# Second layer of a two-layer convolution kernel: branch bias as matmuls, left pooling read from PSUM, one norm for all of c1

## The reference, cut to what matters

```
x = x + L0(_gn(x), ...)
g = _gn(x)                                    # "input norm" of the second layer
p1 = relu(conv3x3(g, p1_w) + p1_b)            # 64 -> 32 channels, branch 1
p2 = relu(conv3x3(g, p2_w) + p2_b)            # 64 -> 32 channels, branch 2
pool1 = cummax(p1, axis=H, reverse=True)      # top pooling
pool2 = cummax(p2, axis=W, reverse=True)      # left pooling
p_gn1 = group_norm(conv3x3(pool1 + pool2, p_w), p_gn_g, p_gn_b)
gn1   = group_norm(conv1x1(g, c1_w), gn1_g, gn1_b)
x = x + relu(conv3x3(relu(p_gn1 + gn1), c2_w) + c2_b)
```

## Time and profile before

| what | value |
|---|---|
| median of 3 runs | 147.26 us (147.07 to 148.74) |
| profiled execution: own time | 146.71 us |
| profiled execution: span, first to last instruction | 144.9 us |
| PE matmul busy | 126.0 us, 87% |
| DVE busy | 109.3 us, 75% |
| ACT busy | 57.2 us, 39% |
| POOL busy | 19.7 us, 14% |
| mean granted clock of TensorE | 0.986 |

### The profile page before, as it was taken

How to read it: one execution, slowest core, us unless ns; L and a number is a source line. 1 busy time by engine, 2 the same in 40 slices (tenths; PEclk the granted TensorE clock), 3 DMA queues, 4 the chain that set the end, 5 groups by cost and what they waited for, 6 DMA issues and landing times.

```text
span 144.9 us, 3074 instructions
## 1 busy us (share of the span) xinstructions
PE 126.0 (87%) x1297; PEld 106.6 (74%) x1297; DVE 109.3 (75%) x197; ACT 57.2 (39%) x101; POOL 19.7 (14%) x27
## 2 busy tenths in 40 slices
PE   4987299999996999999999998899779999788790
PEld 3764199998996989999798987787448576456460
DVE  6529894197489997999999999998575488964601
ACT  4009549859914496045952056001030416030100
POOL 8942330000000000000062000000011001030100
PEclk9999959999999999999999999999999999999999
DMA  3990000039863000000000000000000000000022
GB/s 97 249 185 2 0 0 0 5 105 273 192 137 78 0 2 0 5 0 0 0 5 0 0 0 0 5 0 0 2 0 5 5 5 0 5 0 0 5 72 72
DMA packets 6671, 5.47 MB, mean 38 GB/s; under 512 B 4656, under 2 KB 5938, under 8 KB 6658
## 3 DMA queue, kind: packets, MB, share of 16 engines
q1 hardware_dynamic: 5986, 4.26, 12.4%
q10 hardware_dynamic: 672, 1.02, 2.7%
HBM read 2.85 MB, written 0.52 MB: 23 GB/s over the span
## 4 chain that ended last, share of the span: by engine, by line
PE 50%; DVE 25%; issue 9%; DMA 6%; ACT 3%; POOL 2%; SPq 1%; POOLq 1%; DVEq 0%
PE bank L1017 11%; PE bank L992 9%; PE bank L1042 7%; DVE prod L743 7%; DMA prod<-in_w_off 6%; DVE part L770 3%; DVE x_t L862 3%; PE bank L985 3%; PE bank L983 3%; PE bank L1174 3%; PE bank L1141 3%; PE bank L960 2%; DVE wy L778 2%; DVE pooled L868 2%; PE bank L944 2%
## 5 line engine op out<-in xcount | busy, mean ns | idle before, releaser
L743 DVE TENSOR_TENSOR prod<-hat,wy 128x1440 f32<-128x1440 f32 (+3 forms) x25 | 27.4, 1163 | 0.0
L770 DVE TENSOR_TENSOR part<-v,bank 128x1280 f32<-128x1280 f32 (+3 forms) x20 | 21.7, 1111 | 4.7 <-PE bank L1042 2.1
L1017 PE MATMUL bank<-cst,prod 128*128 128x128 f32 (+3 forms) x189 | 22.4, 273 | 1.1 <-DVE prod L743 1.1
L1042 PE MATMUL bank<-cst,part 128*128 128x128 f32 x168 | 21.1, 275 | 1.8 <-DVE part L770 1.4
L1017 PEld LDWEIGHTS bank<-cst,prod 128*128 128x128 f32 (+3 forms) x189 | 20.7, 132 | 1.8 <-DVE prod L743 1.5
L944 PE MATMUL bank<-ones_r 128*128 128x512 f32 x67 | 19.5, 446 | 2.1 <-POOL w_pair L376 2.1
L1042 PEld LDWEIGHTS bank<-cst,part 128*128 128x128 f32 x168 | 18.6, 140 | 3.5 <-DVE part L770 3.0
L992 PE MATMUL bank<-w_cross,g_cross 128*128 128x432 f32 (+1 forms) x90 | 19.7, 334 | 0.0
L944 PEld LDWEIGHTS bank<-ones_r 128*128 128x128 f32 x67 | 14.1, 218 | 5.2 <-POOL w_pair L376 2.1
L992 PEld LDWEIGHTS bank<-w_cross,g_cross 128*128 128x128 f32 x90 | 15.8, 201 | 0.5
L383 POOL TENSOR_TENSOR ab<-ab,half_pow 128x2 f32<-128x2 f32 (+1 forms) x7 | 6.2, 881 | 55.4 <-DVE ab L606 53.5
(11 more groups left out here) (102 smaller groups left out, 162.8 us busy)
## 6 DMA issues: line engine op xcount, KB each, us to landing
v<-v SPq DMA_DIRECT2D x2, 480.0 KB, 5.9
v<-v SPq DMA_DIRECT2D x2, 448.0 KB, 5.4
prod<-in_w_off ACTq DMA_DIRECT2D x1, 486.0 KB, 6.7
prod<-in_w_off SPq DMA_DIRECT2D x1, 486.0 KB, 8.5
w_s<-in_w SPq DMA_DIRECT2D x4, 72.0 KB, 3.5
wc_s<-in_wc SPq DMA_DIRECT2D x2, 144.0 KB, 3.2
wp_s<-in_wp SPq DMA_DIRECT2D x4, 72.0 KB, 2.9
x_b<-in_x SPq DMA_DIRECT2D x1, 256.0 KB, 4.6
```

What stands on the lines that cost most here:

```text
L743: return nc.vector.tensor_tensor(prod[:, 0:K2 * CELLS * cx].rearrange("p (k q s) -> p q k s", k=K2, s=cx)[:, q0:q0 + nd], hat[:, c % 2, d0 ...
L770: nc.vector.tensor_tensor(part[:, n % PARTS, 0:nd, 0:cv].rearrange("p d (q e) -> p d q e", e=HD), moved, weights.unsqueeze(3).to_broadcast ...
L1017: last = nc.tensor.matmul(out_ps[0:size, b * P:(b + 1) * P], prod[:, at:at + size], ident, start=(b == 0 and t == 0), stop=(b == n - 1 and ...
L1042: last = nc.tensor.matmul(comb_bank[:, j * P:(j + 1) * P], part[:, n % PARTS, d, j * P:(j + 1) * P], ident, start=(m == 0 and d == 0 and j ...
```

## The change

- The branch bias is laid down by PE (`branch_bias`): 16 matmuls of a bias row against ones open the sums of both groups' branch banks, between the two group means of the input norm. `b12_s` becomes a zeroed tile with rows at partitions 0 and 64, filled by four small DMAs instead of one. The convolutions then only add. The ReLU is left to the scan, which starts at 0 and multiplies by 0 at each row.
- DVE scans the left branch (hi) straight from PSUM, image by image; ACT only copies the top branch (lo), transposed, to `tops`. The scans write an image to `lo` or `hi` of `maxima`, so that one addition over 128 partitions makes `pooled`.
- The two norms of c1 become one of four columns, with its group mean in `pool_conv(0)`; ACT squares for it. The statistics of c1 move behind the scans on DVE.
- `group_mean` is made of 64x64 matmuls, and a first pair of them adds EPS to the mean square; `pair_variance` is one TENSOR_SCALAR per column, its scalars in PSUM, instead of three linked steps.
- `both_branches` makes the shift between its two passes over p, and waits per column; the last two columns are stored by SP (lo) and ACT (hi) at once. Warm matmuls: 4 and 2 instead of 5 and 4. The sums of `group_mean` go to other banks.

The core of the diff:

```diff
-WARM_IN = (5, 4, 0)
+WARM_IN = (4, 2)
-G0, G_IN, G_C1, G_P, NORMS = 0, 1, 3, 5, 7
+G0, G_IN, G_C1, G_P, NORMS = 0, 1, 3, 4, 6
...
-            sp.dma_start(b12_s[:, :], b12).then_inc(ld_vec, 16)
+            sp.wait_ge(bias_zero, 2)
+            for row in (0, C):
+                for b in range(2):
+                    sp.dma_start(b12_s[row:row + 1, b * CD:(b + 1) * CD],
+                                 b12[b * C:b * C + CD].rearrange("c o -> o c")).then_inc(ld_vec, 16)
...
-            for n in range(0, HALF, 2):
+            for n in range(HALF):
                 sp.wait_ge(res_ready, n + 1)
-                for half, rows in enumerate((lo, hi)):
-                    sp.dma_start(out_d[n, half], res[rows, n, :]).then_inc(stored, 16)
+                sp.dma_start(out_d[n, 0], res[lo, n, :]).then_inc(stored, 16)
+                if n < DUO:
+                    sp.dma_start(out_d[n, 1], res[hi, n, :]).then_inc(stored, 16)
...
-            branches(0)
-            branches(1)
+            for g in range(2):
+                act.wait_ge(r12_ps, g + 1)
+                nc.scalar.activation(tops[:, g].rearrange("p r (x y) -> p r y x", y=H),
+                                     pair_banks(R12_BANK[g])[lo].rearrange("p r (y x) -> p r y x", x=W),
+                                     ACT.Copy).then_inc(tops_ready, 1)
+            act.wait_ge(stats_ps, G_C1 + 1)
+            nc.scalar.activation(sq[:, G_C1, 0:HALF], pair_stats(G_C1)[:, 2 * HALF:],
+                                 ACT.Square).then_inc(sq_ready, 1)
             affine_c(0)
+            second_input(0)
             affine_c(1)
-            second_input(0)
             second_input(1)
...
-                link(nc.vector.tensor_copy(sq[:, s, 0:DUO], apart))
-                link(nc.vector.tensor_tensor(sq[:, s, 0:DUO], apart, sq[:, s, 0:DUO], ALU.mult))
-                nc.vector.scalar_tensor_tensor(ab[:, s, 1, 0:DUO], means[:, 1], EPS, sq[:, s, 0:DUO],
-                                               ALU.add, ALU.add).then_inc(var_ready, 1)
+                for j in range(cols):
+                    last = nc.vector.tensor_scalar(ab[:, s, 1, j:j + 1], apart[:, j:j + 1], apart[:, j:j + 1],
+                                                   means[:, 1, j:j + 1], ALU.mult, ALU.add)
+                last.then_inc(var_ready, 1)
...
-                for k, b in enumerate((1, 0)):
-                    ve.wait_ge(r12_ready, 2 * g + k + 1)
-                    nc.vector.tensor_tensor_scan(reverse(maxima[:, b].rearrange("p r q -> p (r q)")),
-                                                 reverse(keep[:, :]),
-                                                 reverse(r12[:, b].rearrange("p r q -> p (r q)")), 0.0,
-                                                 ALU.mult, ALU.max).then_inc(scanned, 1)
-                ve.wait_ge(scanned, 2 * (g + 1))
-                for r, rows in enumerate((lo, hi)):
-                    nc.vector.tensor_tensor(pooled[rows, g, 1:H + 1, 1:W + 1],
-                                            maxima[:, 0, r].rearrange("p (x y) -> p y x", y=H),
-                                            rows_cols(maxima[:, 1, r]), ALU.add).then_inc(pooled_ready, 1)
+                ve.wait_ge(r12_ps, g + 1)
+                both = pair_banks(R12_BANK[g])
+                for r, to in enumerate((lo, hi)):
+                    nc.vector.tensor_tensor_scan(reverse(maxima[to, g, 1]), reverse(keep[hi, :]), reverse(both[hi, r]),
+                                                 0.0, ALU.mult, ALU.max).then_inc(scanned, 1)
+                if g:
+                    link(c1_stats(1))
+                    norm_totals(G_C1, HALF)
+                ve.wait_ge(tops_ready, g + 1)
+                for r, to in enumerate((lo, hi)):
+                    nc.vector.tensor_tensor_scan(reverse(maxima[to, g, 0]), reverse(keep[lo, :]), reverse(tops[:, g, r]),
+                                                 0.0, ALU.mult, ALU.max).then_inc(scanned, 1)
+                if g:
+                    c1_variance()
+                ve.wait_ge(scanned, 4 * (g + 1))
+                nc.vector.tensor_tensor(pooled[:, g, 1:H + 1, 1:W + 1],
+                                        maxima[:, g, 0].rearrange("p (x y) -> p y x", y=H),
+                                        rows_cols(maxima[:, g, 1]), ALU.add).then_inc(pooled_ready, 1)
...
+            def branch_bias(g):
+                for r, rows in enumerate((lo, hi)):
+                    for b in range(2):
+                        for k in range(2):
+                            cols = slice(b * C + k * CD, b * C + (k + 1) * CD)
+                            nc.tensor.matmul(bank[R12_BANK[g] + r][cols, 0:HW], b12_s[rows, b * CD:(b + 1) * CD],
+                                             ones[rows, :].to_broadcast([C, HW]), start=True, stop=False)
...
-            pool_conv(0, {})
-            pool_conv(1, {2: G_C1 + 1, 4: G_P})
-            out_conv(0, {4: G_P + 1})
+            pool_conv(0, {5: G_C1})
+            pool_conv(1, {2: G_P})
+            out_conv(0, {3: G_P + 1})
```

More of the change, by code:

```diff
@@ L178, in build @@
         g1 = sb("g1", [P, HALF, PW, PW])
-        keep = sb("keep", [C, DUO * HW])
-        r12 = x_t[:, 0:HALF, :].rearrange("p (b r) q -> p b r q", b=2)
-        maxima = x_t[:, HALF:N, :].rearrange("p (b r) q -> p b r q", b=2)
+        keep = sb("keep", [P, HW])
+        tops = sb("tops", [C, 2, DUO, HW])
+        maxima = sb("maxima", [P, DUO, 2, HW])
         pooled = sb("pooled", [P, 2, PW, PW])
@@ L523, in _ @@
             evacuate(NC - 1)
[L526 to L536, removed]
             def affine_c(g):
-                act.wait_ge(norm_ready, g + 2)
+                act.wait_ge(norm_ready, 2)
                 for r in range(2):
-                    last = nc.scalar.activation(c_aff[:, DUO * g + r, :], pair_banks(C1_BANK[g])[:, r],
-                                                ACT.Identity, bias=ab[:, G_C1 + g, 3, r:r + 1],
-                                                scale=ab[:, G_C1 + g, 2, r:r + 1])
-                last.then_inc(caff_ready, 1)
+                    n = DUO * g + r
+                    nc.scalar.activation(c_aff[:, n, :], pair_banks(C1_BANK[g])[:, r], ACT.Identity,
+                                         bias=ab[:, G_C1, 3, n:n + 1],
+                                         scale=ab[:, G_C1, 2, n:n + 1]).then_inc(caff_ready, 1)
             def second_input(g):
@@ L850, in c1_stats, with c1_variance @@
                 ve.wait_ge(c_ps, g + 1)
-                norm_stats(G_C1 + g, [pair_banks(C1_BANK[g])[:, r] for r in range(2)])
+                for r in range(2):
+                    last = nc.vector.bn_stats(bn[:, G_C1, DUO * g + r, :], pair_banks(C1_BANK[g])[:, r])
+                return last
+            def c1_variance():
+                ve.wait_ge(sq_ready, 1)
+                means = pair_stats(G_C1)[:, 0:2 * HALF].rearrange("p (n t) -> p t n", t=2)
+                nc.vector.tensor_tensor(ab[:, G_C1, 1, 0:HALF], means[:, 1], sq[:, G_C1, 0:HALF],
+                                        ALU.add).then_inc(var_ready, 1)
+                link(nc.vector.tensor_copy(ab[:, G_C1, 0, 0:HALF], means[:, 0]))
             def reverse(ap):
@@ L1117, in _ @@
                 project(y0_banks, far_t, 0, W // 2, far_y)
[L1120 removed]
+            def branch_bias(g):
[5 more added lines that the diff above has]
+                                             ones[rows, :].to_broadcast([C, HW]), start=True, stop=False)
+            keep_warm(WARM_IN[0], bank[3][:, :])
             group_mean(G_IN)
[L1122 removed]
+            pe.wait_ge(ld_vec, 80)
+            for g in range(2):
+                branch_bias(g)
+            keep_warm(WARM_IN[1], bank[3][:, :])
             group_mean(G_IN + 1)
[L1124 removed]
             def image(ap):
```

99 lines of the change are left out of this document (55 added, 44 removed).

## The result

Measured: a median of 142.48 us (142.38 to 142.98, 4 runs) against 147.57 us (147.07 to 148.74, 4 runs) of the kernel before, a ratio of 0.967 with a 95% interval of 0.963 to 0.971. The forecast was 143.0. The profiled execution took 142.55 with a span of 140.8; 142.46 and 140.65 had been worked out.

The account below looks back on a forecast made before the run. The second layer was taken as bound by PE, with DVE's serial chains showing between convolutions. Savings of 3.85 and 0.4 made -4.25: 142.46 us for the profiled run, plus 0.55 to the median, 143.0; range 141.8 to 145.0.

Parts of the forecast that it names:

- Step 1: Input norms before conv(0): shorter group means and variance start conv(0) at about 109.05 instead of 109.39, -0.35 us.
- Steps 2 and 3: Branch convolutions, first pooling: pool_conv(0) can start at 118.4, not 119.26; first pooled image done at 116.4, not 118.68.
- Step 4: Second pooling: PE does not stall; pool_conv(1) starts at 122.95 instead of 124.39, 1.44 us saved, on margins of 0.3.
- Steps 5 and 6: From pool_conv(0) to out_conv(0), 3.05 us saved so far; then between the output convolutions, 3.85 saved so far.
- step 6: Between the output convolutions: mean after 12 instructions, not 16; stall 0.45 instead of 1.02, PE resuming at 132.95.
- Step 7: The end: the last image's two stores go on SP's and ACT's queues instead of ACT's alone, -0.4 us.
- Step 8: The start: three POOL memsets ahead of the warm-up and three more small loads on SP's queue cost nothing.
- The price of PSUM: PSUM as DVE's source: charged nothing; the skill's estimate, 0.065 us more per instruction, would give 143.1 to 143.3.
- Case C: Rival, ahead of conv(0): fewer warm matmuls let the clock halve, doubling both branch convolutions' 9.3 us: 152.3; chance 0.03.

Follow-up runs that it names:

- act_after_scans: Changed kernel, but in the second group ACT's copy of the top waits for DVE's two scans of the left; 142.76 us, ratio 0.971 to before.
- old_stores: Changed kernel with stores divided as before: SP both halves of images 0 and 2, ACT of 1 and 3; 143.08 us, ratio 0.968 to before.
- warm_4_0: Changed kernel with four warm matmuls ahead of the first second-layer input mean and none ahead of the second; 143.27 us, ratio 0.971 to before.
- no_warm: Changed kernel with no warm matmuls around the second layer's input means (0 and 0 instead of 4 and 2); 144.90 us, ratio 0.985 to before.
- old_norm_steps: Changed kernel with group means as two full-array matmuls and variances as three linked DVE steps, as before; 144.87 us, ratio 0.976 to before.

## Why the prediction was right

Step by step, in microseconds after the last projection, so that the 0.12 by which this execution's first layer was ahead does not count:

| | before | forecast | after |
|---|---|---|---|
| conv(0) starts | 5.07 | 4.73 | 4.82 |
| pool_conv(0) starts | 14.94 | 14.08 | 14.00 |
| pool_conv(1) starts | 20.07 | 18.63 | 18.55 |
| out_conv(0) starts | 26.65 | 23.58 | 23.59 |
| out_conv(1) starts | 32.48 | 28.63 | 28.63 |
| span ends | 40.58 | 36.33 | 36.60 |

(Forecast: its times less 104.32.)

- *Step 1* was 0.1 too large. DVE comes to `g` only behind the second statistics and totals, and conv(0) waits until g's second column is written (108.17 to 108.87; conv(0) is released by DVE, 0.20 after PE was free). The second mean is not on that path, so its being 0.1 shorter did not count. The mean (0.45) and the variance (0.56 for 0.55) were right.
- *Steps 2 and 3*: right in the main. The scan is 0.69 and not 0.65, ACT's copy 1.03 and not 1.13; bias and ReLU have left it. The first pooled image has 1.5 us to spare, where two were forecast.
- *Step 4*, the deciding one, held to within 0.1: no stall. But that was closer than it was said to be. Margins of a quarter of a microsecond at c1's mean and 0.3 at the pooled image had been worked out; the trace shows less than 0.1 at either. DVE came 0.1 later than forecast, counted from conv(0), the image at 13.66 instead of 13.55, and PE nearly 0.2 earlier. What softened this lies behind it: PE then waits 0.21 for the statistics of p. Undoing one piece of it at a time gives 0.64 for the copy, 0.63 for the addition, 0.34 for the order and 0.97 for the merged norm. These do not add to a share of the gain, since each starts from a point where PE and DVE meet. Not undone on their own were the bias on PE, the ReLU in the scan, and the new order in `both_branches`; what each is worth is not shown, and the group mean and the variance were undone only together.
- *Steps 5 and 6*: 3.06 and 3.85 saved at the two output convolutions, 3.05 and 3.85 forecast. The stall left before out_conv(1) is 0.58 and not 0.45; PE had reached it 0.1 earlier. The sum of step 6 has a slip in it: from 129.3 its terms give 132.76, not 132.85. That the start of out_conv(1) was met to the hundredth owes something to it.
- *Step 7* was mis-sized: stores bring 0.1 instead of 0.4. I had counted the issues, which do start 0.3 to 0.4 earlier, and not that two queues at once issue and land more slowly. The 0.27 missing at the end is made of that, and the start of this execution, 0.12 ahead, hid part of it in the sum.
- *From the sum to the median.* The sum gave 142.46 for the profiled execution, which took 142.55. The forecast of 143.0 added the 0.55 by which the profiled execution of before lay under its median, and this did not come: the median was 142.48. None of the four runs had the lower mean clock (0.974 to 0.977) that 17 of the 25 runs of the kernel before in the later batches show; act_after_scans, old_stores and warm_4_0, whose tails are the same, have medians of 142.76, 143.08 and 143.27. The change itself is worth 3.85 in the tail and 0.13 behind it, as far as the traces show; the other 1.1 of the 5.09 between the medians is luck with the first layer.
- *Step 8*: nothing showed.
- *The price of PSUM*: the estimate of 0.065 us per instruction, worked out from the cycles in the Trainium skill, "VectorE: DVE Perf Modes", section on the TRN2 errata, does not show: 0.691 and 0.686 for the scan.
- *Case C* did not happen in the changed kernel, but its mechanism is real, and my ground against it was poor: that idle pieces get shorter was true only because four warm matmuls still stood in the first. Its price was wrong as well. A fall costs 2.1 to 2.6 here and not 9.3, since the clock is back before conv(0) ends; it had both convolutions at half speed. With the first constant of WARM_IN at 0 more than half of the gain would have been lost.

## What to carry to other kernels

When PE is nearly full and DVE's chains show only between convolutions, follow the two queues in parallel and note where they meet; a piece taken from the chain is worth most of its duration there (0.64 for a copy of 0.68) and little where there is slack (of an addition of 0.6 in the first pooling, 0.24 showed). Slack is to be read on the engine's whole queue, not on the one result. Moving work that nobody waits for behind work that somebody does cost nothing here. Before thinning out matmuls that only fill time, see which gap they stand in: those in the first long gap keep the clock, later ones may be useless. Where whole times vary from a part that was not touched, compare the distance between two fixed points of the trace.

## What the runs showed of the hardware

- A scan from PSUM costs what it does from SBUF (691 and 686 ns for 64 x 256; all of them run backwards, half of them onto other partitions, and the four from PSUM lie between 689 and 692), and is not slowed by ACT reading the same banks in other partitions at the same time (690 ns either way; ACT's copy 1041 against 1027).
- In no_warm the clock went to half between 106 and 107; PE had worked 0.04 us of 105 to 106 and stood still for 1.38 until 106.42. The clock stayed full in the changed kernel, whose longest piece without work there is 0.28, but also in warm_4_0 with a wait of 0.69 and in the kernel before with one of 0.73.
- Two DMA queues issuing 64 KB stores at the same moment: one issue took 0.825 us instead of 0.62 at most, and ACT's landed after 2.2 to 2.3 instead of 2.0.
- A pause of 0.53 us in PE's weight loads with a full clock, no wait and no DMA packet in flight near it (old_norm_steps) that no trace here explains.
